# Eight batches in two lanes of one core: another table of turns, with the second lane half a batch behind the first

## What is computed

```python
x = x + attn0(ln(x))   # causal softmax attention, 16 heads of 8
x = x + ffn0(ln(x))    # 8 experts, top 2, router with two layernorms
x = x + attn1(ln(x))   # linear attention with 64 relu features a head
x = x + ffn1(ln(x))    # shared expert, and top 1 of 16 routed experts
x = x + attn2(ln(x))   # attention whose scores are masked to a band of 64
x = x + ffn2(ln(x))    # top 4 of 32 sigmoid-gated experts
x = x + attn3(ln(x))   # state-space layer: h = exp(dt*A)*h + dt*u*B, 16x8x48 states
x = x + ffn3(ln(x))    # relu squared, then the count of spikes in 5 steps
```

```python
def step(h, inp):
    dt_t, b_t, c_t, u_t = inp
    a_bar = jnp.exp(dt_t[..., None] * A[None, :, None, :])
    h = a_bar * h + (dt_t * u_t)[..., None] * b_t[:, :, None, :]
    y_t = jnp.einsum('bhds,bhs->bhd', h, c_t)
    return (h, y_t)
```

## Time and profile before

| What | Value |
|---|---|
| Device time, median of 3 runs | 1916.99 us |
| Lowest and highest of the runs | 1910.95 and 1922.92 us |
| Span of the profiled execution, first to last instruction | 1909.3 us |
| Instructions in it | 29013 |

### The profile page before, as it was taken

One profiled execution on the slowest core, in us unless ns is written; L12 is line 12 of the kernel. 1 busy time (PEld: TensorE's weight loads), 2 busy tenths in 40 slices (PEclk: granted clock), 3 DMA queues, 4 the chain that ended last, 5 costly groups with the idle time before them and its releaser, 6 DMA issues.

```text
span 1909.3 us, 29013 instructions
## 1 busy us (share of the span) xinstructions
PE 1602.4 (84%) x10660; PEld 920.5 (48%) x10660; DVE 1267.7 (66%) x2849; ACT 1025.7 (54%) x1967; POOL 791.0 (41%) x734
## 2 busy tenths in 40 slices
PE   6789899867988898987787889996778898999867
PEld 3456664313545676521354567651235456754214
DVE  4655558998554464799865455589975545549995
ACT  4555446655555444665455544466545554455654
POOL 2331215885132112588614220268841422117791
PEclk9999999888999998988899999998789999999789
DMA  6004402020000440212000053021100014302110
GB/s 220 1 1 137 133 16 73 28 89 12 12 1 1 141 134 11 73 40 78 12 12 1 4 162 113 14 71 59 55 12 6 1 40 135 111 18 77 49 46 12
DMA packets 91982, 105.41 MB, mean 55 GB/s; under 512 B 7104, under 2 KB 70336, under 8 KB 91584
## 3 DMA queue, kind: packets, MB, share of 16 engines
q1 hardware_dynamic: 89792, 99.37, 16.9%
q0 software_dynamic: 2048, 4.20, 0.7%
HBM read 80.60 MB, written 22.94 MB: 54 GB/s over the span
## 4 chain that ended last, share of the span: by engine, by line
PE 58%; DVE 20%; ACT 11%; POOL 6%; issue 4%; DMA 1%; DVEq 0%; SPq 0%; ACTq 0%; POOLq 0%
PE P L238 12%; DVE M L2038 7%; PE P L1652 6%; PE P L1881 4%; POOL M L2108 3%; PE P L1233 2%; PE P L406 2%; PE P L978 2%; PE P L2166 2%; DVE st L185 2%; PE P L1238 2%; PE P L1249 2%; DVE M L200 1%; PE P L1660 1%; PE P L1205 1%
## 5 line engine op out<-in xcount | busy, mean ns | idle before, releaser
L2038 DVE TENSOR_TENSOR_SCAN M<-P,M 128x512 f32<-128x512 f32 x384 | 444.9, 1204 | 19.5 <-ACT P L1973 17.8
L1973 ACT ACTIVATE P<-M,negA 128x512 f32<-128x512 f32 x384 | 262.3, 689 | 170.5 <-DVE M L2038 167.9
L1881 PE MATMUL P<-M,wt 32*32 32x512 f32 x3072 | 247.0, 712 | 105.4 <-DVE M L2038 64.3
L238 PEld LDWEIGHTS P<-wt,M 128*128 128x128 f32 x2176 | 278.2, 194 | 100.5 <-issue 43.9
L238 PE MATMUL P<-wt,M 128*128 128x128 f32 x2176 | 292.1, 280 | 10.0 <-ACT M L1980 4.0
L2108 POOL TENSOR_TENSOR M<-M 128x512 f32<-128x512 f32 x192 | 238.6, 1273 | 104.6 <-ACT M L1955 75.0
L2108 POOL TENSOR_TENSOR M<-W,M 128x512 f32<-128x512 f32 x192 | 242.9, 1294 | 62.9 <-PE P L1881 62.8
L1881 PEld LDWEIGHTS P<-M,wt 32*32 32x32 f32 x3072 | 38.9, 111 | 251.1 <-DVE M L2038 156.0
L1749 DVE TENSOR_TENSOR M<-M,P 128x512 f32<-128x512 f32 x128 | 87.0, 682 | 76.7 <-PE P L1660 72.5
L1652 PE MATMUL P<-M,wt 128*128 128x512 f32 x256 | 134.5, 607 | 0.8 <-ACT M L1701 0.5
L1701 ACT ACTIVATE M<-P 128x512 f32<-128x512 f32 x128 | 76.4, 597 | 101.2 <-PE P L1652 92.9
(11 more groups left out here) (352 smaller groups left out, 3225.9 us busy)
## 6 DMA issues: line engine op xcount, KB each, us to landing
W<-in_e SPq DMA_DIRECT2D x88, 192.0 KB, 2.7
M<-in_e SPq DMA_DIRECT2D x64, 192.0 KB, 2.6
M<-dt SPq DMA_DIRECT2D x48, 256.0 KB, 4.4
M<-xs SPq DMA_DIRECT2D x32, 256.0 KB, 3.2
ys<-M SPq DMA_DIRECT2D x32, 256.0 KB, 2.3
W<-du SPq DMA_DIRECT2D x32, 256.0 KB, 4.8
W<-xh SPq DMA_DIRECT2D x16, 256.0 KB
M<-du SPq DMA_DIRECT2D x16, 256.0 KB, 4.2
```

The lines of the kernel that those rows point to most:

```text
L238: m = e.matmul(out[:, tok(j)], h[:, tok(j)], wgt, start=first and j == 0, stop=last, skip_group_check=True)
L1881: m = e.matmul(t["sums"][i // 2][to:to + 32, :], part("WC", c)[r, r], scan[r, :], start=c == 0, stop=c == 5, tile_position=(32 * i, to))
L1973: e.activation(t["aa"][n % 2][:, :], t["dtr"][i][:, :], EXP, scale=negA[:, c:c + 1]).then_inc(ACT.s, ACT.mark(b, "a3", "aa", n))
L2038: e.tensor_tensor_scan(bb[:, :], t["aa"][n % 2][:, :], bb[:, :], 0.0, MUL, ADD).then_inc(DVE.s, DVE.mark(b, "a3", "scan", n))
```

## The change

All five rows of the table of turns are replaced. No instruction is added, removed or altered, and within a lane none changes its place; the number of turns of each engine is the same (2211, 1644, 2247, 682, 191). One line of each of two rows, as the diff has them:

```diff
             "tensor": (2211,
-                "00000111028836dff826fffff50fe4000002113081ee4e30fff17bb3cda2108effc21f25e4cb7600400000000dbc5d6d49fd"
...
+                "41ea2480ece1050815fc29dffcf0f0000009089080fe030f832c70f0e18effe10fd1efe129000000000005f8440fc2000000"
...
             "vector": (2247,
-                "0000003ffa98501ee00000051bfa00773fffbbf2bf8101800012228f53f93ffffb40d186036050c017e8100e3ffc1ffd4924"
...
+                "403f41f001ffc0000001e00a6a18203abfffbef2be910140000004321c0e9f8c7ffffe60c000c0002018c198000040000000"
...
```

More of the change, by code:

```diff
@@ new lines, in program @@
+                "1ef174f448db7ffffe5b3e70203a4000f22af825f29b820203010890ce3d406d501ec7c2003dffff02dffc1fe15171308000"
+                "0936003fff8bf7ab07dedc607fefedde7bdd000fe17cf8498f7fffa7bff740241a4001e82af831f29b822018010221997b40"
+                "6d301e8e3a003dffff8375fc6df841e418080002bc007bfff474c0ffaf6ea07ff7dcef7bdd000ff07cf44999ffff87fff3c0"
+                "241a4003c82af82aff22e08080018090937ac02e983d7b200798ff7fffe1c3fe141eb200000450e0078affff0edaa77ef807"
+                "e8f7dcef7f9e000fa37cfe0c0ffffeffffffffffffffffffffffe"),
@@ new lines, in program @@
+            "scalar": (1644,
+                "50f17000027f4c73e8f980112400599b34c528dbfd10e7108001d380010e0410000000017f32b099f7a308020a5fbfed713f"
+                "dabfecc33392a58a024b36dd0057f03fb73d915730acb7edd80608669cc89003aa2a9973543db3ac267dfa02008527effda8"
+                "d7f757fd9929c8c90d4092cceb6025fcbf19f9d09556272fdeb00410ed4ab52400b684d35aea0fb4eb131f7e44002149fbff"
+                "6b8cffefabecc2a8aa24a022b3dec053adffb076ca57304a8df7db106635f240011207212ae6ad437b3da127ffffffffffff"
+                "fffffffffff"),
```

26 lines of the change are left out of this document (8 added, 18 removed).

## The result

The changed kernel takes 2051.52 us (median of 4 runs, 2050.34 to 2052.66) against 1918.47 us for the kernel before beside it: a ratio of 1.0688, interval 1.0641 to 1.0734. It is 133 us slower. Forecast were 1954 us with a range up to 2010, so the sign was right and the size was not: 97 us are missing, and the time lies outside the range.

The account below looks back on a forecast made before the run. TensorE was taken as busiest (1602.4 of 1909.3 us), with VectorE binding where attn3 overlaps. 268 + 118 + 3 x 458 + 50 + 115 + 19 + 2 = 1946 us of span, plus 8 gives 1954 us; 8-in-10 range 1893 to 2010.

Parts of the forecast that it names:

- Up to batch 0's ffn2: Opening part, to the end of batch 0's ffn2: 268 us, ends 262 and 275, against 269.5 before.
- Attn3 of batch 0: First attn3, beside batch 1's ffn1 and attn2: goes at its own chain's pace, sum 114 us, taken as 118.
- attn3 stretch: Part of a period with one lane in attn3, two per period: 134 us each, ends 114 and 140.
- The pace of 1.63: Time per scan beside a partner of another kind: 1.63 us against 1.24 alone, used for 48 scans.
- The suffix: Part of attn3 after its 48 scans: priced at 24.4 us.
- The rest of the period: Period outside its two attn3 stretches, mostly ffn2, ffn1, attn0, attn2: 181 us of TensorE work at 0.95, 190 us.
- The end: After the last period: batch 7's ffn2 50 us, then lane 1 alone, attn3 115 and ffn3 19, last store 2.
- The price of the ends: First pair's attn3 and the lone last one cost 77 us; three periods give back 40.
- Clearly slower: Rival, chance 0.15: scans wait in VectorE's order behind waiting instructions; stretch 148, rest 201, period 497, time 2071 us.
- No difference: Rival, chance 0.22: mixed stretches run at full clock and TensorE binds them; period 447, time 1921 us.
- faster: Rival, chance 0.18: the recurrence hides wholly; attn3 stretch 118, period 426, time 1858 us.
- The clock: TensorE's granted clock should stay up beside PE-rich layers; gathers 11 us less a pair, none of it counted.

Follow-up runs that it names:

- e1: Kernel after (long lag) with each GpSimd inflow product replaced by two memsets of the same 512 columns: 2002.5 us, ratio 1.0448 to the kernel before.
- e5: Kernel after, same lag and instructions, with all five rows of the order table re-mixed: 2002.9 us, ratio 1.0443 to the kernel before.
- e9: Kernel after with all five rows re-mixed and each inflow product replaced by two memsets: 1989.7 us, ratio 1.0376 to the kernel before.
- e10: Kernel after with each gather matmul issued twice: 2101.3 us, ratio 1.0986 to the kernel before.

## Why the prediction was right and wrong

**Up to batch 0's ffn2**: forecast 268 us, measured 257.9; ten too many.

**Attn3 of batch 0**: forecast 118, measured 134.1. The chain alone was the wrong price already here: the scans took 78.7 us instead of 59.7, beside a partner said to bring little work. A ready scan stood in VectorE's order for 18 us, and 6 us went by waiting for inputs. The two errors cancel to 6 us, which is luck.

**The step that failed is the attn3 stretch**, "29.6 + 48 x 1.63 + 24.4 = 132 us, and I take 134". Measured are 153.2: prefix 29.8, scans at 1.93 us each, suffix 31.1. The term that was mis-sized is what a partner costs: over its chain alone (114 us) the forecast gave it 20 us, and over attn3 alone as measured (105.7 us) it costs 47.5. The pace of 1.63 was taken beside ffn2. The text saw that the new partners bring more VectorE work and added 2 us for it, with no row for the size. The same count over the scans of that row (24 from 1250.8 us in the kernel before) shows what had changed. Per scan, VectorE's other instructions kept a ready scan for 0.42 us beside ffn2 and 0.46 in the new stretches, and an idle VectorE for 0.09 and 0.06: these are alike. What grew is the wait for inputs: 0.1 us for all 24 scans beside ffn2, 11.4 us for 48 now, 9.2 of them for late decays. (Such waits were not foreign to the old table: in batch 2, also beside ffn2, 24 scans from 781.3 us waited 4.0 us for decays.) The forecast looked for the wait on VectorE alone. The suffix was taken at 24.4 us, from a place with only ffn3 beside it, and took 31.1. So of the 21 us over the 132 the scans' window has 14.2, most of it late inputs, and the suffix 6.7.

How much of the 47.5 us can be had back is shown for parts only: contention up to 7.6 (e1, stretch 145.6), another mix 5.6 (e5, 147.6), both together 6.8 (e9, 146.4; these are single profiles). That the rest is waiting in the orders of the engines is read from the trace, and no run took it away.

**The rest of the period**: forecast 190, measured 184 to 188. Right, and by the row that was named for it.

**The end**: forecast 50, 115 and 19; measured 51.6, 105.7 and 19.1. Right in kind; the lone attn3 is shorter, its suffix 20.7 us without any partner.

**The price of the ends** was given as 77 us, and three periods were to give 40 back. The ends cost 60 (568.4 against 507.9), and the periods cost 78 more instead of giving back. The forecast said slower because of the ends alone. That reason holds, at 60 us for 77; the longer periods, the larger part of the loss, it had with the wrong sign.

**The rivals.** "Clearly slower" came nearest, 2071 us; its total is right to 20 us and its point of decision (a stretch above 140) was passed. But its terms were 148 and 201 where 153 and 186 were measured, so that the total is right in part by luck. Its mechanism was named for VectorE, a scan behind an instruction that itself waits. That is 2.9 us of a stretch by the count; the same kind of wait was larger on ScalarE (11.7 us, the part in which it stood idle before a ready decay), where the text did not look, and 9.2 us of late decays reached the scans. "No difference" and "faster" both needed TensorE at 0.90 or more in a period; it reached 0.84, and 0.85 in the kernel before (400.7 of 471.5). That is a check the forecast could have made: 400.7 of work in 458 us is 0.875, more than any period had shown.

**The clock.** The text expected it to stay up beside richer partners and counted nothing. It fell: 0.73 in ffn0 beside attn3, where TensorE works for 35.6 of 63.5 us, and 0.892 over the span. The 0.73 lies between the two levels of 1.2 and 2.4 GHz. For the same matmuls TensorE was busy 60 us longer than in the kernel before. How much of that became time is not shown: e10 raised the clock and lost time, but by adding work.

What stays open: of the 133 us, some 60 are the ends and up to 29 the contention. The other 44, some 15 us in each period, are the lag's, and no run took them apart further; that the kernel before lets two recurrences fill each other's waits is argued from its 125.4 us of VectorE in 138.2, not shown. No other lag was measured.

## What to carry to other kernels

Where two chains take turns in a fixed order, check the sum of a forecast against the busy share that the bounding engine has ever reached over a whole period, and look for waits in the order of every engine that the chain passes, not only of the busiest one; a pace read beside one partner does not hold beside another. A step whose cost vanishes when it is shortened alone is not proof that it is free, nor that a partner hides it: look first at a place where the chain runs alone, and at what sets its pace there. And a lag pays its ends in full (60 us here) before any period can earn them back.

## What the runs showed of the hardware

A 0.19 us VectorE instruction on SBUF tiles takes up to 1.30 us beside GpSimd's products, and not only with two inputs: the one-input lines 766 (0.17 us at the median) and 705 (0.18 in the kernel before) took 0.98 and 1.13 in the same layer. Scans that read an accumulator bank keep their 1.20 us. Without the products the long lag lost 49 us and the short one 20, which bounds what this was worth here.

The granted clock moved with TensorE's own work, against the saving: with a third of the gather work gone (an estimated 85 us) only 47 us of busy time went, and the clock over the span fell from 0.892 to 0.870; doubling the same matmuls (3072 to 6144, busy time up by 128 us) brought 0.940.

The recurrence, alone on the core, kept its length of 105 to 109 us when its scans, decays or gathers were cut, one at a time; it fell to 89.0 us only when the inflow product on GpSimd (1.27 us) was cut with them.
